# Expert loads gated on the first half of an expert's scattered outputs, in a decoder layer on one core

## The reference

```
logits = x @ gate_weight.T                       # only 48 of 128 experts exist
top_v, top_i = top_k(softmax(logits), 8)         # 8 experts a token, weights normalised
xb[e, pos] = x[tok]                              # up to 192 tokens an expert, in order of arrival
gu = einsum('ech,eoh->eco', xb, gate_up_proj)    # 512 -> 2 x 192
h  = silu(g) * u
out = einsum('eci,ehi->ech', h, down_proj)       # 192 -> 512
final = zeros.at[tok].add(out[e, pos] * weight)  # back to the tokens, summed
```

## Time and profile before

| | |
|---|---|
| runs | 1121.84, 1121.9, 1123.8 us |
| profiled execution | 1131.94 us, its span 1130.2 us |
| granted TensorE clock, mean | 0.978 |
| busy over the span: PE, DVE, ACT, POOL | 92%, 77%, 55%, 50% |
| first and last pair issued, expert stage | 739.92 and 1118.66 us of the span |

### The profile page before, as it was taken

The page is one execution under the profiler, slowest core; times in us unless marked ns, Lnnn a source line. Parts: engine busy times, 40 slices in busy tenths (PEclk is TensorE's granted clock), DMA queues, the critical chain, the costliest instruction groups (busy, mean ns, idle before and its releaser), DMA issues.

```text
span 1130.2 us, 24509 instructions
## 1 busy us (share of the span) xinstructions
PE 1042.7 (92%) x6564; PEld 835.2 (74%) x6564; DVE 864.6 (77%) x2382; ACT 621.7 (55%) x1751; POOL 570.6 (50%) x529
## 2 busy tenths in 40 slices
PE   5998899999999999999999987999999999999992
PEld 4776777777777777777777775788777877778771
DVE  5776788878878888888788865387787778787871
ACT  4554445555455455554554542376666667666661
POOL 2114565665666566656656566434444434444343
PEclk9999899999999999999999998899999999999995
DMA  7999474543312113112122120399999999999974
GB/s 294 373 286 289 155 256 156 196 150 119 135 53 91 50 47 93 47 47 92 47 75 65 39 76 11 111 237 248 249 251 245 249 260 243 254 247 260 247 179 55
DMA packets 94052, 185.72 MB, mean 164 GB/s; under 512 B 24791, under 2 KB 24791, under 8 KB 93504
## 3 DMA queue, kind: packets, MB, share of 16 engines
q1 hardware_dynamic: 62640, 145.10, 40.8%
q0 software_dynamic: 31376, 40.20, 17.1%
HBM read 116.00 MB, written 122.00 MB: 211 GB/s over the span
## 4 chain that ended last, share of the span: by engine, by line
PE 48%; DMA 26%; issue 12%; POOL 6%; ACT 4%; DVE 3%; another core or an unknown queue 0%; POOLq 0%; SPq 0%; DVEq 0%; ACTq 0%
DMA layer_out<-qk_both,slot_table 24%; PE ps L1181 23%; PE ps L1166 9%; PE ps L1171 5%; PE ps L1208 3%; POOL layer_out L619 2%; PE ps L1279 2%; PE ps L1312 2%; POOL slot_records L543 2%; ACT heads_t L642 1%; ACT heads_high L640 1%; PE ps L1188 1%; PE ps L1296 1%; DMA gu_sb<-in_weights 1%; PE ps L1337 1%
## 5 line engine op out<-in xcount | busy, mean ns | idle before, releaser
L543 POOL DMA_INDIRECT slot_records<-row,slot_idx x256 | 266.4, 1041 | 90.1 <-issue 60.4
L619 POOL DMA_INDIRECT layer_out<-qk_both,slot_table x96 | 163.3, 1701 | 234.3 <-DMA layer_out<-qk_both,slot_table 204.1
L554 POOL TENSOR_TENSOR rstd<-mv,neg_half 128x1 f32<-128x1 f32 x96 | 79.5, 828 | 132.2 <-DVE mv L914 78.8
L640 ACT ACTIVATE xn_t<-ps 128x512 f32<-128x512 f32 x64 | 38.3, 598 | 138.9 <-PE ps L1166 109.7
L1181 PE MATMUL ps<-w_high,xn_high 128*128 128x512 f32 x384 | 114.1, 419 | 0.7 <-ACT xn_high L640 0.7
L1337 PE MATMUL ps<-w_high 128*128 128x192 f32 x576 | 91.2, 280 | 19.5 <-DVE w_low L1088 17.5
L1181 PE MATMUL ps<-w_low,xn_high 128*128 128x512 f32 x384 | 108.5, 405 | 0.0
L1181 PE MATMUL ps<-w_high,xn_low 128*128 128x512 f32 x384 | 107.2, 401 | 0.0
L1337 PEld LDWEIGHTS ps<-w_high 128*128 128x128 f32 x576 | 76.4, 192 | 40.0 <-issue 39.3
L675 ACT ACTIVATE probs<-ps,neg_max_s 128x128 f32<-128x128 f32 x256 | 89.8, 377 | 19.4 <-DVE neg_max_s L911 19.4
L1088 DVE TENSOR_TENSOR w_low<-gu_sb,w_high 128x1536 fp32r<-128x1536 f32 x48 | 84.4, 1757 | 11.9 <-ACT w_high L640 9.1
(11 more groups left out here) (164 smaller groups left out, 2431.4 us busy)
## 6 DMA issues: line engine op xcount, KB each, us to landing
gu_sb<-in_gate_up SPq DMA_DIRECT2D x48, 768.0 KB
slot_records<-dn_both SPq DMA_DIRECT2D x6, 3366.0 KB, 20.7
w_raw<-slot_records SPq DMA_DIRECT2D x48, 280.5 KB
dn_both<-in_down_proj SPq DMA_DIRECT2D x48, 256.0 KB
x_ln<-in_x SPq DMA_DIRECT2D x32, 256.0 KB
x_res<-in_x SPq DMA_DIRECT2D x32, 256.0 KB
ctx_t_sb<-in_ctx_t SPq DMA_DIRECT2D x32, 256.0 KB
ctx_sb<-in_ctx_rows SPq DMA_DIRECT2D x32, 256.0 KB
```

Source lines behind the costliest of these rows:

```text
L543: pool.indirect_dma_start(out=records, out_offset=bass.IndirectOffsetOnAxis(ap=slot_idx[:, s.parity, k:k + 1], axis=0), in_=row[:, s.parit ...
L554: pool.tensor_tensor(rstd[:, :], mv[:, 1:2], neg_half[:, 0:1], ALU.pow).then_inc(steps.sem, 1)
L619: pool.indirect_dma_start(out=out, out_offset=bass.IndirectOffsetOnAxis(ap=slot_table[0:PART[h], 2 * d.index + h:2 * d.index + h + 1], axi ...
L640: act.activation(dst, src, ACT.Copy).then_inc(steps.sem, 1)
```

## The change

SyncE's loop over the experts is written out. After the first few loads, each of its turns waits for the first half of expert n's outputs to have landed, and then loads rows of n+4, gate-up of n+5 and down of n+3, where the loop before was held back by the buffers alone. For this the two halves signal separate semaphores (`d_add[half][parity]`); all waits on them follow: GpSimd waits for both halves of the expert before, one after the other, ScalarE for half 0 of the expert two before, VectorE for half 1.

```diff
-        d_add = [sem("outputs_added0"), sem("outputs_added1")]
+        d_add = [[sem(f"outputs_of_half{h}_added{n}") for n in range(2)] for h in range(2)]
...
-            load_gate_up(Batch(1, 0, E))
-            with sp.Fori(1, E // 2 - 1) as pair:
-                for off in range(2):
-                    load_rows(Batch(pair, off, E))
-                    load_gate_up(Batch(pair, off + 1, E))
-                    load_down(Batch(pair, off, E))
-            load_rows(Batch(E // 2 - 1, 0, E))
-            load_gate_up(Batch(E // 2 - 1, 1, E))
-            load_down(Batch(E // 2 - 1, 0, E))
-            load_rows(Batch(E // 2 - 1, 1, E))
-            load_down(Batch(E // 2 - 1, 1, E))
+            def expert(n):
+                return Batch(n // 2, n % 2, E)
+            load_gate_up(expert(2))
+            load_rows(expert(2))
+            load_gate_up(expert(3))
+            load_down(expert(2))
+            load_rows(expert(3))
+            load_gate_up(expert(4))
+            for n in range(E - 3):
+
+                sp.wait_ge(d_add[0][n % 2], moved(expert(n), 1))
+                if n + 4 < E:
+                    load_rows(expert(n + 4))
+                if n + 5 < E:
+                    load_gate_up(expert(n + 5))
+                load_down(expert(n + 3))
             for par in range(2):
-                sp.wait_ge(d_add[par], 16 * 2 * E // 2)
+                for h in range(2):
+                    sp.wait_ge(d_add[h][par], 16 * E // 2)
...
-                    compute_op=ALU.add).then_inc(d_add[d.parity], 16)
+                    compute_op=ALU.add).then_inc(d_add[h][d.parity], 16)
...
-                    pool.wait_ge(d_add[d.back(1).parity], moved(d.back(1), 2))
+                    pool.wait_ge(d_add[1][d.back(1).parity], moved(d.back(1), 1))
+                    pool.wait_ge(d_add[0][d.back(1).parity], moved(d.back(1), 1))
...
-                        act.wait_ge(d_add[d.back(2).parity], moved(d.back(2), 2))
+                        act.wait_ge(d_add[0][d.back(2).parity], moved(d.back(2), 1))
...
-                        dve.wait_ge(d_add[d.back(2).parity], moved(d.back(2), 2))
+                        dve.wait_ge(d_add[1][d.back(2).parity], moved(d.back(2), 1))
```

## The result

The changed kernel takes 1207.4 us (median; 1203.5 to 1210.5) against 1122.3 us for the kernel before on the same chip (1121.8 to 1123.8): a ratio of 1.0754, 95% interval 1.072 to 1.0787. It is 85 us slower where 8 us less were forecast, and lies far outside the range. The profiled execution is the one of 1203.48 us, with a span of 1201.8.

What follows compares the result with a forecast made beforehand. The expert stage was taken as bound by full DMA engines at 8.0 us a turn: 6.6 + 43 x 8.0 + 6.6 + 2 x 6.34 + 0.9 = 370.8 us against 378.74, hence 1114.0 us, range 1093 to 1130.

Steps and rivals of the forecast that it cites:

- The gate: SyncE's loads wait for half 0, landing at 5.0 us; second add undisturbed, next first add meets at most 1.3 us.
- prediction's own two reasons for being wrong: Stated in advance: the cost per byte changes with the order of loads, or `y` is late for GpSimd.
- The larger of the two sums: A steady expert turn costs the larger of DMA engine time, 5.28 + 2.72 = 8.0 us, and the adds' chain, 7.6.
- The chain of the adds: Successive add pairs in the expert stage: 6.34 us undisturbed plus at most 1.3 us of loads, 7.6 a turn.
- Rival B: Adds without company waste the DMA engines: turn 8.4 us, 1131 us in all, share below 0.95 as sign; chance 0.22.
- The semaphores: ScalarE's wait for `y` ends at half 0 and shrinks, off the chain; GpSimd's extra waits cost 0.9 us.
- SyncE's loop written out: Issue work on SyncE, an engine that waits 5 us in each turn: costs nothing.
- The start: First spacings of the expert stage: one batch per pair, spacing 0 about 6.6 us, later steady 8.0, everything one expert later.
- The computing engines: TensorE, VectorE and ScalarE lose their loads' lead, but `y` is ready 3.5 us before GpSimd wants it: costs nothing.

Runs made afterwards that it cites:

- e16: e17 with each gate-up load as four transfers instead of one: 1111.4 us, ratio 0.9866.
- e8: The kernel before with each gate-up load as four transfers of 192 KB: 1116.4 us, ratio 0.9911.
- e17: e2 with shared semaphores for the halves, batches released by a GpSimd memset behind the second add instead of half 0's landing: 1115.4 us, ratio 0.9921.
- e13: e9 with ScalarE again waiting for both halves of the expert two before: 1127.9 us, ratio 1.002.
- e10: The kernel before with only SyncE's expert loop written out, old order, shared semaphore: 1139.3 us, ratio 1.007.
- e7: e4 with the semaphore raised by the end of a small GpSimd memset behind the second add: 1135.2 us, ratio 1.0088.
- e15: e9 with VectorE's splits of the down weights waiting for a GpSimd memset behind both adds' descriptors: 1144.5 us, ratio 1.0152.
- e12: e11 with each gate-up load as four transfers: 1158.7 us, ratio 1.0209.
- e3: The changed kernel with each 768 KB gate-up load as four transfers of 192 KB: 1162.3 us, ratio 1.0346.
- e11: e5 with gate-up of n+6 waiting for a GpSimd memset behind the second add of pair n: 1173.2 us, ratio 1.0375.
- e6: The changed kernel with its gate, but each batch in the old order (down, rows, gate-up): 1190.8 us, ratio 1.0573.
- e18: The changed kernel with shared semaphores, its batch waiting for the landing of the whole pair instead of half 0: 1193.7 us, ratio 1.0598.
- e2: The changed kernel with the same gate releasing loads one expert further ahead (rows n+5, gate-up n+6, down n+4): 1200.2 us, ratio 1.0688.
- e14: The changed kernel with ScalarE waiting for both halves of the expert two before: 1206.0 us, ratio 1.073.
- e9: The kernel before with only the semaphores of the two halves split and the waits on them changed: 1240.9 us, ratio 1.0968.
- e1: The changed kernel without SyncE's new wait; written-out loop, load order and split semaphores stay: 1249.2 us, ratio 1.1026.
- e5: The changed kernel without the gate and with the old load order; written-out loop and split semaphores stay: 1254.5 us, ratio 1.1156.
- e4: e2 with the batch waiting for a semaphore increment GpSimd issues behind the second add's instruction, instead of half 0's landing: 1245.4 us, ratio 1.1063.

## Why the prediction was wrong

All runs in one table, by ratio. The columns are medians over the pairs from 780 to 1080 us of each timeline, in us behind the pair's first issue: when gate-up is issued (the first of its parts, where it is in four), and when the second add's instruction ends.

| kernel | gate-up | second add's descriptors | ratio |
|---|---|---|---|
| e16, shared, behind marker, in four | 4.7 | 3.7 | 0.987 |
| e8, before, in four | 5.2 | 3.7 | 0.991 |
| e17, shared, behind marker | 4.8 | 3.7 | 0.992 |
| before | 5.2 | 3.7 | 1 |
| e13, split, ScalarE as before | 5.2 | 3.8 | 1.002 |
| e10, loop only | 4.7 | 3.7 | 1.007 |
| e7, split, behind marker | 6.1 | 5.0 | 1.009 |
| e15, splits behind marker | 7.8 | 3.3 | 1.015 |
| e12, gate-up behind marker, in four | 5.2 | 5.0 | 1.021 |
| e3, gate, in four | -0.5 | 4.6 | 1.035 |
| e11, gate-up behind marker | 5.2 | 5.0 | 1.038 |
| e6, gate, old order | 0.5 | 4.5 | 1.057 |
| e18, gate on the whole pair | 0.6 | 3.6 | 1.060 |
| e2, gate, one ahead | 0.0 | 3.3 | 1.069 |
| e14, gate, ScalarE as before | 0.0 | 3.6 | 1.073 |
| after | 0.0 | 3.6 | 1.075 |
| e9, split only | 4.7 | 5.0 | 1.097 |
| e1, e5 | 3.8, 3.9 | 5.0 | 1.103, 1.116 |
| e4 | 3.8 | 5.0 | 1.106 |

Where gate-up is issued behind the second add's descriptors the ratio is at most 1.04. Where it is ahead of them, it is at least 1.057, but for e3, which cuts the load up.

**The gate: this step failed.** Half 0 "lands between 4.2 and 6.07. I take 5.0", and so "the second add is not disturbed by its own turn's loads any more", and the next first add gets "at most these 1.3" us of loads. The size was right for an undisturbed pair: 5.16 measured beside pair 0. But it was used for every turn, where half 0's landing is itself moved by the loads that it releases. It settled at a median of 9.0 us in place of 5.0, and from then on it was rows and gate-up whole, 5.0 us of packets, that stood ahead of the first add, not 1.3. e2 and e7 show this step by itself: with the same batches and semaphores, 1200.2 us at the gate and 1135.2 behind the adds. That e17 comes out at 1115.4 us, near the forecast 1114, is luck: it is another kernel, with shared semaphores and batches one expert ahead. Neither of the prediction's own two reasons for being wrong explains the loss: the engines' time for a turn's bytes hardly changed (7.85 us against 8.0), and `y` wasn't late for GpSimd in the steady stretch.

**The larger of the two sums: this failed with it.** "The engines have their own sum, and the larger of the two counts." The sum held (7.85 against 8.0), in part by luck: its loads were 0.35 us too low and its adds 0.50 too high. The chain of the adds, put at 7.6, was 10.05 and became the larger. When a large load is served first and the adds come after it with little beside them, the two times follow one another: 4.97 us at 91% and 4.33 at 76%, and then the engines wait for the next issue. Rival B had a piece of that (adds without company) and its sign, a DMA share below 0.95, but priced a turn at 8.4 and put the idle time between the second add and the rows.

**The semaphores: costed wrongly by 111 us (1240.9 against 1129.9 in e9's comparison), though the gate hid it.** ScalarE's shorter wait was to be "off the chain". The wait did go away. But it had been what kept VectorE's splits, and the loads that hang on them, behind GpSimd's issues. e9 and e13 show this step by itself; e7 and e11, with issues as long or nearly and gate-up behind them, show that the loads' new place is most of its price, and e15 that VectorE's work is what makes the issues long. In the changed kernel it adds nothing to the gate's price (e14), but taking only the gate away is no cure for this reason (e1).

**SyncE's loop written out** was "nothing" and is 0.7% by itself (e10). That this comes from gate-up's issue, 0.5 us sooner in the median, is not shown.

**The start.** That "everything is one expert later" and an even spacing from the start came true in part: no spacing of 12.8 is left, but spacing 0 was 7.80, not 6.6, as `y` of expert 1 came late from ScalarE, and the last three are 7.81, 7.14 and 6.29 in place of 6.6 and 6.34.

**The computing engines** were costed at nothing with 3.5 us to spare for `y`. In the steady stretch GpSimd waits for landings, not for `y` (265.5 us against 8.5 from 740 on), so this held, though at a turn 2 us longer than forecast.

What stays open: why e9 and e5 are worse than the gate, with gate-up at 4.7 and 3.9 rather than in front of both adds. In e9 the DMA engines are in use for 0.73 of the time from 780 to 1070 us, and serve 3 packets in the first 2.3 us behind the pair at 885.16. That the loads are then done and wait for VectorE, which waits for the landing, is read from the timeline; no run takes it apart. Open too is why e11 still costs 3.8% with gate-up behind the descriptors: its rows and down loads go out 2.8 and 1.8 us behind the pair, ahead of them.

## What to carry to other kernels

Here the landing of a transfer was a poor release for the next transfers on the same engines, since they delayed that very landing. Release loads by something upstream of the contention (here the end of the second add's descriptor making), and work the cycle through two or three turns until the times repeat, before the sum is made. Before a wait is shortened as harmless, ask which engine it keeps out of whose way: follow everything that starts sooner, two engines further on. And where a small transfer on the critical path shares the DMA engines with a large one, look at which is issued first: that was worth 6% here, and cutting the large one up made it matter less.

## What the runs showed of the hardware

- Two queues did not share the engines evenly when a 768 KB load had been issued first: 4.97 us with 389 packets of the one and none of the other. With the load in four, 37 packets of the other came through in the same time. The Trainium skill, page "DMA: Bandwidth & Descriptors", section "Queues, rings and completion order", says that an engine alternates between queues but drains a whole packet, of many descriptors, before it switches. The runs agree with that if a load's share of an engine is one such unit; what the page calls a packet no row here shows.
- An increment behind an indirect add on GpSimd fired when the add began (SyncE's rows went out at 890.05, the add's instruction ran from 890.07 to 892.92), while a memset behind it ended 0.12 us behind the add's end. Between the two lay 110 us.
- The issues of the adds of 128 and 64 rows took 1.55 and 1.42 us at best and up to 2.53 and 2.86 in e9, longer or shorter with what VectorE did beside them; the mean over both was 2363 ns in e9 and 1528 in e15.
- TensorE's granted clock was 0.88 in the mean over the steady stretch of the changed kernel, where TensorE waited for loads, and stood at 1.00 in e17 and before. The 10.05 us turn has 8.6 us of busy TensorE in it, so this did not set the time.
